# Causal softmax attention in fp32: the rows are divided by their sums before the transposes, the copies are shared out anew, and the output projection moves to the transposes' banks

## The reference

```python
q = (x @ Wq).reshape(b, n, H, DH)            # x is layernormed; b=2, n=2048, H=16, DH=64
k = (x @ Wk).reshape(b, n, H, DH)
v = (x @ Wv).reshape(b, n, H, DH)
bias = slope[:, None, None] * (pos[:, None] - pos[None, :])
scores = jnp.einsum('bihd,bjhd->bhij', q, k) * scale + bias[None]
scores = jnp.where(causal[None, None], scores, jnp.float32(-1e+30))
attn = jax.nn.softmax(scores, axis=-1)
out = jnp.einsum('bhij,bjhd->bihd', attn, v).reshape(b, n, H * DH)
x = x + out @ Wo + bo
```

## Time and profile before

| | |
|---|---|
| median of 3 runs | 6423.55 us (6419.34 to 6424.36) |
| the profiled execution | 6422.4 us, of which the span from first to last instruction is 6420.6 us |
| busy over the span | PE 4151.8 us, DVE 4477.1 us, ACT 4424.7 us, POOL 1418.0 us |
| the stage that changes | first scores at 68.9 us, last addition to X at 2625.95 us |
| one pair in the middle | 160.2 us from one bias to the next |

### The profile page before, as it was taken

How to read it: one execution, slowest core, us unless ns; L and a number is a source line. 1 busy time by engine, 2 the same in 40 slices (tenths; PEclk the granted TensorE clock), 3 DMA queues, 4 the chain that set the end, 5 groups by cost and what they waited for, 6 DMA issues and landing times. The chain is left out here.

```text
span 6420.6 us, 71259 instructions
## 1 busy us (share of the span) xinstructions
PE 4151.8 (65%) x22532; PEld 1927.3 (30%) x22532; DVE 4477.1 (70%) x7016; ACT 4424.7 (69%) x3439; POOL 1418.0 (22%) x1211
## 2 busy tenths in 40 slices
PE   6888888888888888744454545454544545454446
PEld 4555555555555555521011111110310101111104
DVE  5555555555545555559898898986599898989865
ACT  3444444444444444328999999999289999999992
POOL 0000000000000000004444444442044444444420
PEclk9999999999999999866676677776766777767767
DMA  1000000000000000028888888887288889888871
GB/s 33 5 5 5 5 5 5 4 5 5 5 5 5 5 5 2 3 74 168 186 184 181 184 179 186 186 179 157 102 165 184 182 184 188 176 187 185 181 158 56
DMA packets 137164, 628.41 MB, mean 98 GB/s; under 512 B 28038, under 2 KB 66120, under 8 KB 66632
## 3 DMA queue, kind: packets, MB, share of 16 engines
q0 software_dynamic: 73728, 536.90, 41.7%
q1 hardware_dynamic: 63048, 86.55, 3.9%
HBM read 65.30 MB, written 21.23 MB: 13 GB/s over the span
## 5 line engine op out<-in xcount | busy, mean ns | idle before, releaser
L1244 DVE SCALAR_TENSOR_TENSOR b_tiles<-b_ra_rep,b_cap,psum 128x1024 f32<-128x1024 f32 x1024 | 1260.4, 1270 | 248.4 <-PE psum L1475 235.0
L562 DVE CUSTOM_DVE_ANT_0 a_srow<-psum,a_bias 128x512 f32<-128x512 f32 (+3 forms) x1280 | 729.0, 607 | 554.9 <-PE psum L732 527.2
L1475 PE MATMUL psum<-b_qT,b_kT 126*128 126x512 bf16 x2048 | 766.8, 486 | 499.5 <-DVE b_tiles L1244 496.0
L635 ACT ACTIVATE a_pT<-psum 128x512 f32<-128x512 f32 (+3 forms) x848 | 439.8, 548 | 926.4 <-PE psum L743 924.1
L1488 PE MATMUL psum<-b_tiles,b_v_aug 128*32 128x512 f32 x2464 | 449.4, 814 | 681.2 <-ACT b_tiles L1388 681.1
L1251 DVE TENSOR_SCALAR b_tiles<-b_tiles 128x2048 f32<-128x2048 f32 x512 | 667.1, 1303 | 5.5
L732 PE MATMUL psum<-a_k,a_q 64*128 64x512 f32 (+3 forms) x2560 | 637.2, 576 | 36.1 <-DVE a_cmax L562 22.2
L743 PE MATMUL psum<-ident,a_srow 128*128 128x128 f32 x4352 | 615.9, 280 | 44.2 <-ACT a_pT L635 36.9
L648 ACT ACTIVATE a_srow<-a_srow,a_nmax 128x1536 f32<-128x1536 f32 (+15 forms) x512 | 610.3, 1198 | 33.1 <-DVE a_nmax L568 30.1
L199 POOL MEMSET ffn_rank<- 128x1 f32 x16 | 0.7, 99 | 2701.2 <-POOLq L74 2701.2
L1388 ACT ACTIVATE b_tiles<-b_tiles,b_sc 128x4096 f32<-128x4096 f32 x154 | 585.5, 3802 | 5.1
(11 more groups left out here) (213 smaller groups left out, 5936.7 us busy)
## 6 DMA issues: line engine op xcount, KB each, us to landing
b_tiles<-b_tiles POOLq DMA_DIRECT2D x308, 1024.0 KB, 12.5
X<-b_tiles POOLq DMA_DIRECT2D x204, 1024.0 KB, 13.0
b_ra_rep<-ra_scratch SPq DMA_DIRECT2D x32, 1024.0 KB, 6.6
x_scratch<-X SPq DMA_DIRECT2D x8, 1024.0 KB, 10.5
kv_scratch<-b_tiles SPq DMA_DIRECT2D x4, 2048.0 KB, 8.8
X<-x_scratch SPq DMA_DIRECT2D x8, 1024.0 KB, 9.4
X<-in_x_dram SPq DMA_DIRECT2D x4, 1024.0 KB, 9.7
a_wqk<-in_wqk_dram SPq DMA_DIRECT2D x32, 128.0 KB, 2.6
```

Source lines behind the costliest of these rows:

```text
L562: nc.vector.tensor_tensor_reduce(out=srow[:, n % ROWS, h, a:z], in0=bank(c % 2 * 2 + h, 0, z - a), in1=bias[:, h, off + a:off + z], scale= ...
L1244: nc.vector.scalar_tensor_tensor(out=a[:, s * HALF:(s + 1) * HALF], in0=ra_rep[:, j, s * HALF:(s + 1) * HALF], scalar=cap[:, j, k:k + 1], ...
L1475: last = nc.tensor.matmul(half_ps(s)[:, i * BANK:(i + 1) * BANK], kT[:, j, k * P:(k + 1) * P], qT[:, j, cs], start=True, stop=True)
```

## The change

Each half-row is now divided by its sum on VectorE in place, between its exponential and its transposes (`invert`: one reciprocal of a column, one multiplication of the whole half-row). With that `zrep`, its transposes, `zT` and the multiplication into `oT` are gone; ScalarE copies the product to `oT` (a piece "C", at the end of each even step). The product with V comes in parts of four key tiles, placed between scores and transposes. The transposes now go by key group, both heads one after the other. The values' pieces are spread over steps 0 and 1. The output projection takes a place in the ring of three banks, which now has 92 entries a pair: 80 blocks of transposes, 4 of values, 8 projections. VectorE reads all projections and every sixth entry of the ring, 14 of the 84 copies (28 before); ScalarE makes the other 70 (56 before). The first scores of a pair no longer wait for all of q.

```diff
 def order(n):
-    t = [("T", i) for i in range(len(blocks[n - LAG]))] if 0 <= n - LAG < TB else []
-    if n == 0:
-        x = [("V", i) for i in range(NVE)]
-    if n >= 4:
-        x = [("O", (n - 5) // 2) if n % 2 else ("A", (n - 4) // 2)]
+    m, k = n - LAG, (n - 4) // 2
+    t = [("T", i) for i in range(len(groups[m]))] if 0 <= m < TB else []
+    a = [("A", i) for i in range(len(parts[k]))] if n >= 4 and n % 2 == 0 else []
+    seq = []
+    for i in range(max(len(s), len(t), len(a), 1)):
+        seq += s[i:i + 1]
+        if i == 0 and n >= 5 and n % 2:
+            seq += [("O", k)]
+        seq += a[i:i + 1] + t[i:i + 1]
+        if n < 2 and i % 2:
+            seq += [("V", 2 * n + i // 2)]
+    if a:
+        seq += [("C", k)]
+    if n >= TB:
+        seq += [("P", 2 * (n - TB)), ("P", 2 * (n - TB) + 1)]
...
-on_dve = [e % 3 == 2 for e in range(NEV)]
+on_dve = [entry[0] == "O" or e % 6 == 5 for e, entry in enumerate(ring)]
...
 # VectorE, body; m = n - 1
+def invert(m, h):
+    dve.wait_ge(exp_done, (g * TB + m) * 2 + h + 1)
+    nc.vector.reciprocal(zinv[:, m, h:h + 1], zsum[:, m, h:h + 1]).then_inc(zinv_done, 1)
+    dve.wait_ge(zinv_done, (g * TB + m) * 2 + h + 1)
+    row = srow[:, m % ROWS, h, 0:(tiles[m] + 1) * P]
+    nc.vector.tensor_scalar(row, row, zinv[:, m, h:h + 1], None, ALU.mult).then_inc(scaled, 1)
...
+        if 0 <= m < TB and j == (len(seq) - 1) // 2:
+            invert(m, 0)
     if 0 <= m < TB:
-        nc.vector.reciprocal(zinv[:, m, :], zsum[:, m, :]).then_inc(zinv_done, 1)
-        dve.wait_ge(zT_done, g * NIB + max(m // 2 - 1, 0))
-        nc.vector.tensor_copy(zrep[:, m % 4, :, :], zinv[:, m, :].unsqueeze(2).to_broadcast([P, 2, DH])
+        invert(m, 1)
...
-        nc.vector.tensor_tensor(oT[:, k % 2, :], bank(6, 0, IB), zT[:, :], ALU.mult).then_inc(oT_done, 1)
...
 # ScalarE, body
+if what == "C":
+    act.wait_ge(av_done, g * NPA + part0[i + 1])
...
+    copy(oT[:, i % 2, :], bank(6, 0, IB)).then_inc(oT_done, 1)
...
 # TensorE
 def scores(g, n, i):
     if c == 0:
-        pe.wait_ge(q_copied, (g + 1) * 4)
         pe.wait_ge(k_copied, (g + 1) * 4)
+        pe.wait_ge(q_copied, g * 4 + 2)
+    if c == 1:
+        pe.wait_ge(q_copied, (g + 1) * 4)
...
 def transposes(g, n, i):
-    if i == 0 or h != blocks[n][i - 1][0]:
-        pe.wait_ge(exp_done, (g * TB + n) * 2 + h + 1)
-    evacuated(pe, g, e - 3)
+    a, z = groups[n][i]
+    for h in range(2):
+        e = place["T", n, i, h]
+        if i == 0:
+            pe.wait_ge(scaled, (g * TB + n) * 2 + h + 1)
+        bank_free(pe, g, e)
...
 def out_projection(g, k):
     pe.wait_ge(oT_done, g * NIB + k + 1)
+    e = place["O", k]
+    bank_free(pe, g, e)
-        last = nc.tensor.matmul(bank(6, i * IB, (i + 1) * IB), oT[:, k % 2, i * P:(i + 1) * P], wo_sb[:, :],
+        last = nc.tensor.matmul(bank(T_BANKS[e % 3], i * IB, (i + 1) * IB), oT[:, k % 2, i * P:(i + 1) * P],
```

More of the change, by code:

```diff
@@ L388, in stage_attn_a @@
     NVE = 4
-    blocks = [[(h, a, min(a + 4, it + 1)) for h in range(2) for a in range(0, it + 1, 4)] for it in tiles]
-    evac0 = [NVE + sum(len(c) for c in blocks[:n]) for n in range(TB + 1)]
-    NEV = evac0[TB]
+    groups = [[(a, min(a + 4, it + 1)) for a in range(0, it + 1, 4)] for it in tiles]
+    parts = [[(a, min(a + 4, 2 * ib + 2)) for a in range(0, 2 * ib + 2, 4)] for ib in reversed(range(NIB))]
+    part0 = [sum(len(c) for c in parts[:k]) for k in range(NIB + 1)]
+    NPA = part0[NIB]
     ROWS = 3
@@ L396, in stage_attn_a, with order @@
     NPR = len(PROJ)
-    on_dve = [e % 3 == 2 for e in range(NEV)]
+    def order(n):
+        m, k = n - LAG, (n - 4) // 2
+        s = [("S", i) for i in range(len(slots[n]))] if n < TB else []
+        t = [("T", i) for i in range(len(groups[m]))] if 0 <= m < TB else []
[12 more added lines that the diff above has]
+            seq += [("P", 2 * (n - TB)), ("P", 2 * (n - TB) + 1)]
+        return seq
+    ring = []
+    for n in range(STEPS):
+        for what, i in order(n):
+            ring += {"T": [("T", n - LAG, i, 0), ("T", n - LAG, i, 1)], "V": [("V", i)], "O": [("O", i)]}.get(what, [])
+    NEV = len(ring)
+    place = {entry: e for e, entry in enumerate(ring)}
+    on_dve = [entry[0] == "O" or e % 6 == 5 for e, entry in enumerate(ring)]
+    tile_end = [place["T", n, len(groups[n]) - 1, 1] + 1 for n in range(TB)]
     def count(upto):
@@ L708, in values @@
                     pe.wait_ge(wv_loaded, (g + 1) * 16)
[L709 to L714 removed]
+                e = place["V", i]
+                bank_free(pe, g, e)
+                ps = bank(T_BANKS[e % 3])
                 for t in range(4):
@@ new lines, in transposes @@
+                for h in range(2):
+                    e = place["T", n, i, h]
+                    if i == 0:
+                        pe.wait_ge(scaled, (g * TB + n) * 2 + h + 1)
+                    bank_free(pe, g, e)
+                    for jt in range(a, z):
+                        last = nc.tensor.transpose(bank(T_BANKS[e % 3], (jt - a) * P, (jt - a + 1) * P),
+                                                   srow[:, n % ROWS, h, jt * P:(jt + 1) * P], env.ident[:, :])
+                    last.then_inc(bank_done, 1)
@@ L763, in product_with_v @@
+            def product_with_v(g, k, i):
+                ib = NIB - 1 - k
+                if i == 0:
+                    e = tile_end[2 * k + 1]
+                    pe.wait_ge(dve_evac, g * n_dve + count(e))
+                    pe.wait_ge(act_evac, g * n_act + e - count(e))
+                    pe.wait_ge(oT_done, g * NIB + k)
+                    pe.sem_inc(passed, 1)
+                for jt in range(*parts[k][i]):
                     lo = P if jt == 2 * ib + 1 else 0
```

146 lines of the change are left out of this document (55 added, 91 removed).

## The result

The changed kernel takes 6134.2 us (median of 4 runs, 6132.4 to 6138.5) against 6422.6 us in the same session: a ratio of 0.9553, 95% interval 0.9536 to 0.9569. It is 288 us faster, where 235 were forecast. The last addition to X starts at 2338.0 us, before at 2625.9: the whole gain lies in this stage.

The account below looks back on a forecast made before the run. TensorE was taken as the bound, losing time at waits. Terms gave -13.9 us a pair, plus -1.7 for the clock in 12 regular pairs and -10 for last pairs: 235 us off 6422.4, so 6187 us, range 6120 to 6300.

Parts of the forecast that it names:

- rival A: Whole stage: the gains and losses as summed, 6187 us, range 6150 to 6240; chance 0.57.
- B: Whole stage: TensorE hardly waits at all; with half the new waits, 3.6 us a pair better, 6130 us; chance 0.11.
- The transposes of `zrep`: Ahead of the product: they leave TensorE, -5.1 us a pair; the wait for X there goes too, -4.7.
- The projection's wait: Before the output projection: 9.0 us a pair for `oT` shrinks to 1.5 as ScalarE alone copies, -7.5 us.
- The head: Start of a pair: q's wait goes, -0.8 us; steps 0 and 1 share the values, -1.6; together -2.4.
- Joins: TensorE's changes between kinds of work: 12 more parts of the product with V, nearly 0.2 us each, +2.4 us a pair.
- VectorE: Its new division work: net +11.8 us a pair, to about 92.5 us, not the bound on the mean.
- The walk: Step-by-step estimate of TensorE's waits for division and copies: 1.0 us in step 2, 0.9 in step 3, 0.4 in step 5.
- The clock: Behind step 17's 3.72 us wait: the clock's fall goes with the wait, -1.7 us in 12 regular pairs.
- C: Ten long steps: VectorE late again and again, 0.7 us each, 7 us a pair lost, 6299 us; chance 0.21.
- D: Eight odd steps: short stops make the clock fall, 1.7 us each, 6405 us, counted as no change; chance 0.03.
- E: Steps 2 to 15: ScalarE's exponentials ahead of its copies become the brake, about 6500 us, slower; chance 0.08.

Follow-up runs that it names:

- the old head: Changed kernel with all four pieces of values in step 0 again and a pair's first scores waiting for all of q: 6209.8 us.

## Why the prediction was right, and where not

The forecast, faster by 235 us with a range of 6120 to 6300, held: 6134 us, 288 faster. Its middle did not. The time lies outside the 6150 to 6240 of rival A, the sum, and on the 6130 of B, which has half of A's new waits. By its mechanism it is neither: TensorE's idle time fell by 1.7 us a pair more than in A, where B has 3.6, and TensorE's work fell by 1.6 more than forecast. That these two make B's time is chance. A pair of 141.3 us is also shorter than the 143 to 147 that were to show A.

From first scores to first scores, 14 of the 16 pairs gained 18.9 us each, where 15.6 were forecast: 46 more. The last pair of each sequence gained 11.6 and 10.8 us (176.3 and 164.8 up to the next sequence's first scores, 140.4 and 129.7 up to the last addition to X), where 10 were forecast: 2 more. The two first pairs were taken to have no fall of the clock, but have the 3.72 us wait and the fall like the others, as at 209.3 us: 3 more. And 1 us lies ahead of the stage's first scores. Together these are the 53 us that were missing. By the parts of the prediction:

1. **The transposes of `zrep`** went, as counted. **The wait for X** went too, but by another cause than the one named. "Since the projection has its own bank" failed: in bank 6 the time is the same, and in the kernel before, moving the addition alone takes the wait away. The prediction read a shared bank in the code and did not ask when VectorE would get to the addition in the new order.

2. **The projection's wait.** Forecast 1.5 us a pair after the change, measured none among TensorE's waits. The term was right in kind and 1.5 us too careful.

3. **The head.** Forecast -2.4 us. Steps 0 and 1 take 16.6 us and not 16.0. The 0.8 us for q only moved to a wait for VectorE in step 0, so that they are worth nothing. The spread was sized too small: 1.6 us, where it is worth 2.7 in the kernel before and 3.8 in the changed one, in which without it the first division falls into step 1. The forecast left out what the spread does to step 2.

4. **Joins.** Forecast +2.4 us, at 0.2 us for each of 12 more parts. With the product in one run TensorE is busy 1.0 us less, so they cost 0.08 each. TensorE's busy time fell by 4.3 us at a full clock (139.6 to 135.4), and -5.1 and +1.0 make -4.1. The 0.2 us were read at changes between scores and transposes, and no run compares such a change with one to the product.

5. **VectorE.** Its work was sized well (93.5 us for 92.5). That it stays off the path is shown from both sides: with the multiplication nearly gone 9 us are gained, doubled it costs 150. The walk's waits came out as forecast in kind: 1.1 us for ScalarE's copies in step 2 (1.0), 0.6 for the division in step 3 (0.9) and 0.3 at the last tile (0.3), 0.7 of the product for a copy in step 16 (0.8, and 0.45 in step 14, which is not seen), 1.9 for late copies of VectorE (2.0). The last is luck in part: the forecast put them behind multiplications, and most of the time they stand behind readings of scores and the addition to X. The 0.4 us of step 5 is 0.1, and the 0.7 us of scores for VectorE in step 0 was not in the walk.

6. **The clock.** Pairs with and without the fall, 160.2 and 158.5 us, bear the 1.7 us out, and the changed kernel's regular pairs have none. The fall hangs mostly on the wait of step 17: with 1.34 us none stands behind it, but 3 of 12 regular pairs have one elsewhere. One of the 12 pairs from which the forecast took 1.7 us is the one at 158.5 us, which had nothing to give.

C's price, 7 us a pair, is near what doubling the work costs in waits (6.6 in the pair shown). D was not seen in the changed kernel, but its mechanism is real: with the work doubled the clock is 0.97, and with the old head it is 0.98 in one of the two sequences. E is refuted: with all copies on ScalarE the kernel is faster.

## What to carry to other kernels

A wait at a shared bank is first a question of when its reader's engine gets to it in its own order; try the reader's place before a new bank. Work put on an engine with slack costs little only if the order leaves it room at the place where its result is wanted: here spreading the values over two steps was worth 2.7 us a pair without the division and 3.8 with it. A wait that is taken away can come back a few instructions later, as q's did, so look for it in the trace of the changed kernel. Edits that share a cause, here it seems the clock, need not add up. Before a large change is credited, take its edits of order alone: they made 167 of these 288 us. Copies out of a short ring belong on the engine that reaches them soonest in its own order, here ScalarE and not VectorE with its readings of scores, and on that engine ahead of work that is wanted a step later.

## What the runs showed of the hardware

Like waits do not always bring the clock down: with the old head one sequence ran at a granted clock of 1.00 (144.9 us a pair) and the other at 0.98 (146.7 us), and in the kernel before 11 of 14 waits of 3.72 us had a fall right behind them. What sets them apart was not tried.

A multiplication by a column is 58 to 61 ns longer than by a constant, whatever the width, in the kernel that does both on the same rows:

```profile
L582 DVE TENSOR_SCALAR a_srow<-a_srow,a_zinv 128x2048 f32<-128x2048 f32 x32 | 41.2, 1286 | 1.1
L584 DVE TENSOR_SCALAR a_srow<-a_srow 128x2048 f32<-128x2048 f32 x32 | 39.3, 1227 | 1.1
...
L582 DVE TENSOR_SCALAR a_srow<-a_srow,a_zinv 128x512 f32<-128x512 f32 x32 | 15.6, 486 | 1.1
...
L584 DVE TENSOR_SCALAR a_srow<-a_srow 128x512 f32<-128x512 f32 x32 | 13.7, 427 | 1.1
```
